# A pre-LN attention and mixture-of-experts layer on one core: the last key tile's product with the values in plain fp32

## The reference, cut to what matters

```
x = x + attention(layernorm(x))        # x: 2 batches, 1024 tokens, 256 features
x = x + experts(layernorm(x))          # 32 experts, 8 a token, and a shared one

k, q, v = W_K x, W_Q x, W_V x          # 16 heads of 128
attn = softmax(causal(k q) / sqrt(128))
z = attn @ v ;  out = W_O z            # in float32
```

## Time and profile before

| | us |
|---|---|
| median of 3 runs | 1352.23 (1350.67 to 1354.55) |
| the profiled execution | 1349.91 |
| its span, first to last instruction | 1347.1 |
| TensorE busy | 1293.7 |
| VectorE busy | 911.5 |
| ScalarE busy | 740.2 |
| GpSimd busy | 570.5 |
| mean granted TensorE clock | 0.992 of full |

### The profile page before, as it was taken

The page is one execution under the profiler, slowest core; times in us unless marked ns, Lnnn a source line. Parts: engine busy times, 40 slices in busy tenths (PEclk is TensorE's granted clock), DMA queues, the critical chain, the costliest instruction groups (busy, mean ns, idle before and its releaser), DMA issues.

```text
span 1347.1 us, 28918 instructions
## 1 busy us (share of the span) xinstructions
PE 1293.7 (96%) x8374; PEld 1159.4 (86%) x8374; DVE 911.5 (68%) x2133; ACT 740.2 (55%) x1688; POOL 570.5 (42%) x585
## 2 busy tenths in 40 slices
PE   7999999999999899999889999999989998999998
PEld 6898888989889797878778988988868997999996
DVE  5667666776766968677887676676668642356645
ACT  2556555565555555555546555555545654556653
POOL 5536545264330404031225545363000764656664
PEclk8999999999999999999999999999999998999999
DMA  3252645526352101000001111111156998899973
GB/s 123 87 180 87 204 145 178 179 86 200 127 191 97 28 5 29 5 28 5 28 7 69 51 63 58 40 47 59 64 188 226 327 322 322 281 328 398 374 237 114
DMA packets 124792, 188.12 MB, mean 140 GB/s; under 512 B 10016, under 2 KB 97824, under 8 KB 124704
## 3 DMA queue, kind: packets, MB, share of 16 engines
q1 hardware_dynamic: 61024, 101.91, 22.6%
q10 hardware_dynamic: 51392, 51.52, 11.3%
q0 software_dynamic: 12288, 33.57, 7.2%
HBM read 107.79 MB, written 87.03 MB: 145 GB/s over the span
## 4 chain that ended last, share of the span: by engine, by line
PE 75%; DVE 9%; issue 7%; ACT 4%; DMA 3%; ACTq 0%; SPq 0%; POOL 0%; DVEq 0%; POOLq 0%
PE ps_t L863 8%; PE ps_s L808 7%; PE ps_s L810 7%; PE ps_s L809 7%; PE ps_x L808 6%; PE ps_x L809 5%; PE ps_x L810 5%; PE ps_z L808 4%; PE ps_z L810 4%; PE ps_z L809 4%; PE ps_t L1028 3%; PE ps_z L1028 3%; PE ps_s L997 3%; DMA ring_down<-experts_dram 3%; PE ps_t L808 2%
## 5 line engine op out<-in xcount | busy, mean ns | idle before, releaser
L1140 ACT ACTIVATE prob<-prob,neg_max 128x128 f32<-128x128 f32 (+7 forms) x256 | 198.6, 776 | 244.6 <-DVE neg_max L1338 244.3
L1355 DVE TENSOR_TENSOR pT_lo<-ps_t,pT_hi 128x512 fp32r<-128x512 f32 (+2 forms) x320 | 189.7, 604 | 101.3 <-ACT pT_hi L1155 97.2
L1155 ACT ACTIVATE pT_hi<-ps_t 128x512 fp32r<-128x512 f32 (+2 forms) x320 | 161.2, 532 | 91.2 <-PE ps_t L863 91.1
L1338 DVE CUSTOM_DVE_ANT_0 prob<-ps_s,later_keys 128x128 f32<-128x128 f32 (+7 forms) x256 | 186.0, 749 | 3.3 <-PE ps_s L810 2.0
L863 PE MATMUL ps_t<-ident,prob 128*128 128x128 f32 x1152 | 171.9, 275 | 12.5 <-ACT prob L1140 5.5
L703 POOL DMA_INDIRECT xs<-xn,slots x128 | 127.8, 998 | 124.2 <-PE ps_z L1028 61.2
L863 PEld LDWEIGHTS ps_t<-ident,prob 128*128 128x128 f32 x1152 | 136.2, 140 | 39.2 <-DVE pT_lo L1355 6.7
L808 PE MATMUL ps_s<-k_hi,q_hi 128*128 128x512 f32 (+2 forms) x384 | 141.2, 368 | 1.0 <-DVE k_lo L1331 1.0
L618 POOL TENSOR_TENSOR a_hi<-raw_a,zero 128x512 fp32r<-128x512 f32 x32 | 33.3, 1041 | 239.8 <-PE ps_x L810 156.0
L808 PE MATMUL ps_s<-ring,a_hi 128*128 x384 | 125.9, 328 | 6.7 <-SPq L549 6.6
L810 PE MATMUL ps_s<-k_hi,q_lo 128*128 128x512 f32 (+2 forms) x384 | 131.9, 344 | 0.0
(11 more groups left out here) (307 smaller groups left out, 3621.8 us busy)
## 6 DMA issues: line engine op xcount, KB each, us to landing
ring<-ws SPq DMA_DIRECT2D x56, 512.0 KB, 5.3
xs<-taken SPq DMA_DIRECT2D x16, 1536.0 KB, 9.8
xq<-xs ACTq DMA_DIRECT2D x48, 512.0 KB, 6.1
xs<-yq ACTq DMA_DIRECT2D x48, 512.0 KB, 6.0
ws<-split_to SPq DMA_DIRECT2D x34, 512.0 KB, 3.2
raw<-experts_dram SPq DMA_DIRECT2D x34, 256.0 KB, 3.3
raw_a<-w_a_dram SPq DMA_DIRECT2D x15, 512.0 KB, 3.6
ring_down<-experts_dram SPq DMA_DIRECT2D x56, 128.0 KB, 6.3
```

The source lines that it names most:

```text
L1140: act.activation(to, to, ACT.Exp, scale=-1.0, bias=neg_max[:, r:r + 1], accum_out=row_sum[:, c, j:j + 1]).then_inc(s_exp, 1)
L1155: act.activation(to, ps_t[m % 2][:, j * P:], ACT.Copy).then_inc(s_hi, 1)
L1338: dve.tensor_tensor_reduce(prob[r // BC][:, r % BC, 0:width(r)], ps_s[r % 2][:, first:first + width(r)], later_keys[:, S - width(r):], 1.0 ...
L1355: dve.tensor_tensor(lo, ps_t[m % 2][:, j * P:], hi.bitcast(F32), ALU.subtract).then_inc(s_bank_free, 1)
```

## The change

The last key tile of each block of four goes unsplit. Its transposed probabilities are copied by VectorE alone, straight from the bank into pL (128 x 128, fp32), and ScalarE has no part in that tile; VectorE takes over ScalarE's two waits (the transposes, and the product three back). The product is one plain fp32 matmul on 128 columns, with unsplit values as weights: v_raw for head 1, and for head 0 a new copy v_last, which ScalarE writes in v parts 1 and 3. The split of v leaves out tile 7, for head 0 in part 3 and for head 1 in split_v1. The memsets of pL_hi and pL_lo go, and the counts of the constants and of s_hi are lower by what has gone.

```
-        pL_hi, pL_lo = [sb(w, [P, 2 * P], F32R, attention) for w in ("pL_hi", "pL_lo")]
+        pL, v_last = sb("pL", [P, P], F32, attention), sb("v_last", [P, 2, DH], F32, attention)
...
-        pool.memset(pL_hi[:, 0:P].bitcast(F32), 0.0).then_inc(s_const, 1)
-        pool.memset(pL_lo[:, 0:P].bitcast(F32), 0.0).then_inc(s_const, 1)
...
-            split(flat(v_hi[1]), flat(v_lo[1]), flat(v_raw), count, s_v1)
+            whole = slice(0, (NT - 1) * DH)
+            split(flat(v_hi[1])[:, whole], flat(v_lo[1])[:, whole], flat(v_raw)[:, whole], count, s_v1)
...
             diag = max(n - c * BC, 0)
+            q0 = diag * P
             if diag == BC - 1:
-                m_hi, m_lo, q0 = pL_hi[:, :], pL_lo[:, :], (BC - 2) * P
+                whole = v_last[:, c, :] if a == 0 else v_raw[:, n, :]
+                pe.matmul(ps_z[:, q0:], whole, pL[:, :], start=False, stop=True).then_inc(s_pv, 1)
             else:
-                q0 = diag * P
-                m_hi, m_lo = pT_hi[t % 3][:, q0:], pT_lo[t % 3][:, q0:]
-            three(ps_z[:, q0:], v_hi[a][:, n, :], v_lo[a][:, n, :], m_hi, m_lo, n == 0,
-                  n == (c + 1) * BC - 1).then_inc(s_pv, 1)
+                three(ps_z[:, q0:], v_hi[a][:, n, :], v_lo[a][:, n, :], pT_hi[t % 3][:, q0:],
+                      pT_lo[t % 3][:, q0:], n == 0, False).then_inc(s_pv, 1)
...
                 act.activation(v_raw[:, t, :], src[:, 1], ACT.Copy)
-                act.activation(v_hi[0][:, t, :], src[:, 0], ACT.Copy).then_inc(s_x_hi, 1)
+                if part % 2:
+                    act.activation(v_last[:, part // 2, :], src[:, 0, 1], ACT.Copy)
+                split = 2 * part + 2 - (part == NT // 2 - 1)
+                act.activation(v_hi[0][:, 2 * part:split, :], src[:, 0, 0:split - 2 * part],
+                               ACT.Copy).then_inc(s_x_hi, 1)
...
-                j = max(n - c * BC, 0)
-                to = pL_hi[:, P:] if j == BC - 1 else pT_hi[t % 3][:, j * P:]
-                act.activation(to, ps_t[m % 2][:, j * P:], ACT.Copy).then_inc(s_hi, 1)
+                act.activation(pT_hi[t % 3][:, j * P:], ps_t[m % 2][:, j * P:], ACT.Copy).then_inc(s_hi, 1)
...
-                hi = pL_hi[:, P:] if j == BC - 1 else pT_hi[t % 3][:, j * P:]
-                lo = pL_lo[:, P:] if j == BC - 1 else pT_lo[t % 3][:, j * P:]
-                dve.wait_ge(s_hi, p * TRS + t + 1)
+                if j == BC - 1:
+                    dve.wait_ge(s_bank, p * BANKED + m + 1)
+                    dve.wait_ge(s_pv, p * TRS + t + PV0 - 2)
+                    dve.tensor_copy(pL[:, :], ps_t[m % 2][:, j * P:]).then_inc(s_bank_free, 1)
+                    return
+                dve.wait_ge(s_hi, p * (TRS - 2 * NC) + t - k + 1)
+                hi, lo = pT_hi[t % 3][:, j * P:], pT_lo[t % 3][:, j * P:]
```

More of the change, by code:

```diff
@@ L465, in build @@
     WS0, YS0 = 16, 16
-    CONSTS = 23 + WORD
+    CONSTS = 21 + WORD
     X_SCORES = [X0 + x_before + count_of(order, ("M", b, 0)) + 1
@@ L670, in _ @@
         pool.iota(thr_int, pattern=[[P, NT]], base=0, channel_multiplier=0).then_inc(s_const, 1)
-        pool.wait_ge(s_const, 16 + 1 + WORD)
+        pool.wait_ge(s_const, 14 + 1 + WORD)
         pool.tensor_copy(number[:, :], number_int).then_inc(s_const, 1)
@@ L1149, in attend @@
             elif kind == "T":
-                t = t_count(k, n)
+                t, j = t_count(k, n), max(n - c * BC, 0)
+                if j == BC - 1:
+                    return
                 act.wait_ge(s_bank, p * BANKED + m + 1)
                 act.wait_ge(s_pv, p * TRS + t + PV0 - 2)
-                j = max(n - c * BC, 0)
-                to = pL_hi[:, P:] if j == BC - 1 else pT_hi[t % 3][:, j * P:]
-                act.activation(to, ps_t[m % 2][:, j * P:], ACT.Copy).then_inc(s_hi, 1)
+                act.activation(pT_hi[t % 3][:, j * P:], ps_t[m % 2][:, j * P:], ACT.Copy).then_inc(s_hi, 1)
             elif kind == "V" and n == (c + 1) * BC - 1:
@@ L1320, in project @@
                 src = bank[:, :].rearrange("p (t a h) -> p a t h", t=2, a=2)
-                t = slice(2 * part, 2 * part + 2)
-                dve.tensor_tensor(v_lo[0][:, t, :], src[:, 0], v_hi[0][:, t, :].bitcast(F32),
+                n = 2 - (part == NT // 2 - 1)
+                t = slice(2 * part, 2 * part + n)
+                dve.tensor_tensor(v_lo[0][:, t, :], src[:, 0, 0:n], v_hi[0][:, t, :].bitcast(F32),
                                   ALU.subtract).then_inc(s_x_free, 1)
```

## The result

The changed kernel takes 1344.7 us (median; 1342.5 to 1346.8), the kernel before in the same rounds 1352.3 us (1350.4 to 1354.6): a ratio of 0.9944, 95% interval 0.9931 to 0.9958, so 7.6 us faster. Forecast were 1344.1 us and a saving of 8.1. The size is right to half a microsecond, but terms of the sum are off in opposite directions, and the experiments were made to find them.

The account below looks back on a forecast made before the run. TensorE's instruction stream was taken to set the time of plain pairs, VectorE's late chains part of the other five. Savings of 6.2 + 1.4 + 0.5 = 8.1 us off the median 1352.2 gave 1344.1 us, range 1341.0 to 1349.0.

Parts of the forecast that it names:

- The product's price: TensorE, last tile's product: two fp32 records of 0.108 us, 0.216 in place of 0.356, saving 0.14 at 64 places.
- The bound with exposed loads: TensorE, last tile's product: each weight load as long as its record, nothing under it, 0.38 us, a loss of 0.024.
- the rival at 0.436: TensorE, last tile's product: each record takes load plus stream, 5.1 us more in all, 1357.3; chance 0.04.
- The dearer halves of 0.16: TensorE, last tile's product: loads don't quite hide, 0.32 us a product, saving 2.3 us in all, 1349.9; chance 0.07.
- So plain pairs keep all four: Eleven plain pairs: all four products' savings of 0.14 us are kept, 6.2 us in all.
- ScalarE's v_last at nothing: ScalarE, v parts 1 and 3: the added copy is hidden in part 1 and "nothing to speak of" at part 3.
- stays and eats nothing: Gap of 0.2 to 0.3 us before T1.0: starts from scores behind X11, so it stays and takes no saving.
- The first rival: Plain pairs: late results lose 0.2 to 0.3 us before X2, W3.0 or T1.0; saving 3 to 5.5 us; chance 0.13.
- VectorE's copy: VectorE, last tile: copy of 0.28 us replaces the 0.287 subtraction, waiting for TensorE's transposes and the product three back, not ScalarE.
- pL_hi's going: Behind V0.3: without pL_hi on ScalarE, k_hi and k_lo come 0.15 us earlier, so X2 follows.
- The other five pairs: MIDDLE, ROUTE, slot and dispatch pairs, LAST: half of 2.8 us kept, 1.4, plus 0.5 for earlier pT and k_lo chains.

Follow-up runs that it names:

- e5: Changed kernel with the last tile's fp32 product issued twice; ratio to the kernel before 1.0014, plain pair 57.58 us.
- e6: Kernel before, but its last tile's three split products work on 128 columns instead of 256; ratio to the kernel before 0.9992.
- e7: Changed kernel, but the fp32 product works on 256 columns, the first 128 of pL being zeros; ratio to the kernel before 1.0032.
- e1: Changed kernel, but ScalarE copies the last tile to pL and VectorE rewrites one column and frees the bank; ratio to the kernel before 0.9977.
- e2: Changed kernel, but VectorE instead of ScalarE writes v_last, in front of v_lo; ratio to the kernel before 0.9929, plain pair 56.81 us.
- e11: Kernel before, unchanged, profiled a second time in one run without a ratio; plain pair 57.32 us, attention 917.21 us.
- e9: Changed kernel run again without edits; ratio to the kernel before 0.9948, 1344.7 us.
- e3: Changed kernel with V0.3 moved in front of T1.0, in MIDDLE and ROUTE too; ratio to the kernel before 0.9933, plain pair 56.82 us.
- e8: Kernel before with only V0.3 moved in front of T1.0; ratio to the unmoved kernel before 1.0018, plain pair 57.64 us.

## Why the prediction was right, and where not

**The product's price** was right: 0.22 us at V1.7, one more for 0.22 in e5, two records each. The bound with exposed loads (0.38, and the rival at 0.436) is out. That rival came from the rule of the Trainium skill, "TensorE: Matmul & The Clock Gate", Part 3, "What overlaps and what doesn't". Here loads into the same full array do overlap: with 0.19 us of record each, they start 0.11 us apart while TensorE goes on with matmuls (e6), and fp32 products of two loads each follow at 0.22. The dearer halves of 0.16 are out too. The prediction took 0.108 as half of 0.215 and asked whether the load would be the floor instead; e7 shows the columns at 256 and e6 the load at 128 on split operands, so at 128 columns of fp32 both are about 0.11; a narrower one was not tried.

**"So plain pairs keep all four"** is the step that failed: the forecast was 11 x 0.56 = 6.2 us, the traces give 11 x 0.40 = 4.4. At V0.3 the reasoning looked at X2 and at T1.1's bank and found that both move along; it looked for z_lo only behind V3.7, at W3.0, and never behind V0.3, at W0.0. There the time from T1.0 is set by ScalarE's and VectorE's results, k_lo and then z_lo, and a shorter V0.3 gives nothing: 3.62 us with the product twice, 3.63 with it once (e5), and with the old chain of copies nothing of its saving is left at the end of the pair (e1).

**ScalarE's v_last at nothing** was mis-sized: 0.10 us a plain pair by e2, about 1.1 us of the eleven, since it delays the first pT_hi of the next pair on the chain that ends in front of T1.0.

Of T1.0 the prediction said that the gap "stays and eats nothing". That holds as far as TensorE's savings go: no last product stands between the scores of row 7 (R0.3) and T1.0, and with products twice as dear the gap is the same (e5). It grew from 0.34 to 0.39 us by v_last.

So a plain pair adds up to: 0.38 us from three products (0.13 each, where 0.14 was forecast), nothing from V0.3, 0.06 to 0.08 lost at T1.0, and 0.08 gained by VectorE's direct copy, which lets k_lo and z_lo come earlier (e1): 0.40. That it comes so near to the three savings is chance, as the last two terms cancel.

The first rival had the mechanism, a result that comes late in a plain pair, and put too much on it: one saving in four was lost, not half. Of its three places W3.0 lost nothing, X2 loses only with the old chain back (e1), T1.0 lost by v_last, and W0.0 it did not name.

**VectorE's copy** was right in length (0.282) and in whom it waits for. That pL_hi's going lets k_hi and k_lo come earlier, and X2 with them, was right in direction, and e1 gives its worth in plain pairs, 0.08 us. The sum had no such term in plain pairs, since it took it as what makes V0.3's saving count.

**The other five pairs** were forecast to give 1.9 us (1.4 and 0.5). The five periods of the table fell by 3.5 in the first two profiles, but 1.5 of it is ROUTE at a lower clock in the profile before; against e11 the two profiles of the changed kernel give 2.0 and 2.5. They hold half of pair 6 and half of pair 11, which are plain (0.4 together). LAST adds about 0.6: its two stretches give 0.5 and 0.3, 0.2 of that by the half of plain pair 14. So the five pairs give 2.2 to 2.7 us, a little more than forecast. With the clock taken off the ROUTE period it is 2.7 in both pairs of profiles, and parted by e1's one profile in the same way about 1.8 of it is the product and 0.9 VectorE's direct copy (an estimate): both above the 1.4 and 0.5 of the forecast, and the product the larger, as forecast.

**The sum.** 4.4 and 2.2 to 2.7 make 6.6 to 7.1 us, where 6.2 and 1.9 made 8.1; that the first timing missed the forecast by only 0.5 us is in part luck. Attention as a whole fell by 7.8 us in the first pair of profiles, 1.5 of it by the clock, and by 7.1 from e11 to e9; the two timings say 7.6 and 7.0. The span of the profiled execution fell by 4.2 us only, since the part behind attention took 2.8 us longer in it (table), in code that is the same, and the part ahead of V1.7 of pair 0 0.9 longer (62.8 to 63.7; the second profile of the kernel before has 63.7 there too).

## What to carry to other kernels

When an engine is 96% busy, its few remaining waits are worth as much study as its work. What is saved on it between the start of a chain on other engines and the wait that ends the chain is given back there (V0.3, between T1.0 and W0.0), so count the savings stretch by stretch between such waits; and put no new copy on such a chain, however short (v_last: 0.06 us by its records, 0.10 a pair in fact). In these rows a narrow matmul had two floors, columns and weight loads: one plain fp32 product of 128 columns (0.22 us) beats three split ones (0.33), and at 256 columns it loses (0.43 against 0.36). An operation that another engine's queue no longer has to pass through can open a place in the order that was closed before (e3 against e8): after such a change, try the order again.

## What the runs showed that was not expected

TensorE's clock behind attention. A window of the changed kernel in the expert part, columns as above:

```profile
1132.00:1136.00 4.00, 3.30 (x15) 3.31 (x16) 0.00 (x0) 0.34 (x1) 0.96 (x1) 0.58 0.82 257
```

and the timeline behind its start:

```profile
1132.70 0.58 PE L807 MATMUL ps_s<-ring,a_hi 128*128 x1 [2.11 <-SPq L549]
1133.08 0.42 PE L808 MATMUL ps_s<-ring,a_hi 128*128 x1
1133.29 0.42 PE L809 MATMUL ps_s<-ring,a_lo 128*128 x1
```

TensorE has waited 2.11 us for a weight transfer, and behind that the granted clock is near the 1.2 GHz level: matmuls that otherwise start 0.12 us apart come every 0.21. Such stretches differ from one profile to the next, and with them the time behind attention: 365.7 us at a mean granted clock of 0.988 there (the kernel before) to 371.6 at 0.978 (e9), over thirteen profiles of code that is the same there. The spread of 5.9 us is near the whole effect of the change, so a single profile's span was no measure of these edits.

The starts of loads (0.11 us apart) and their records (0.19 us) are two things throughout: a record's length is no price, for a matmul or a load.
